# First context's projections between the halves of the last output product, and its keys' softmax ahead of the last gate

## The reference

```
x = layernorm(x + rwkv(x))              # 4 layers: time mix (wkv recurrence), then channel mix
x = layernorm(x + attention(x, ctx))    # 16 heads of 16 channels, no T x S matrix
x = layernorm(x + experts(x))           # 8 experts, dense, weighted by two softmaxes

# channel mix of a layer
kf = square(relu(xk @ Wck.T));  x = x + sigmoid(xr @ Wcr.T) * (kf @ Wcv.T)

# attention
q = softmax(heads(x @ Wq.T + bq));  k = softmax(heads(ctx @ Wk.T + bk));  v = heads(ctx @ Wv.T + bv)
kv = k.T @ v;  D_inv = 1 / sum(q * sum(k))
out = (q + (q @ kv) * D_inv) @ Wp.T + bp
```

## Time and profile before

| | us |
|---|---|
| median of 3 runs | 1799.88 |
| lowest and highest | 1799.08, 1801.06 |
| the profiled execution | 1800.33 |
| its span in the profile | 1798.3 |
| busy in the span: PE, DVE, ACT | 1711.9, 1222.4, 981.0 |

### The profile page before, as it was taken

The page is one execution under the profiler, slowest core; times in us unless marked ns, Lnnn a source line. Parts: engine busy times, 40 slices in busy tenths (PEclk is TensorE's granted clock), DMA queues, the critical chain, the costliest instruction groups (busy, mean ns, idle before and its releaser), DMA issues.

```text
span 1798.3 us, 25765 instructions
## 1 busy us (share of the span) xinstructions
PE 1711.9 (95%) x9740; PEld 1467.2 (82%) x9740; DVE 1222.4 (68%) x1900; ACT 981.0 (55%) x1514; POOL 17.5 (1%) x41
## 2 busy tenths in 40 slices
PE   3699999999999998999999999999999999999997
PEld 1377777778777787988899988999899989998897
DVE  7999999999999857998544444545444444444455
ACT  5788998898999873444533333333333333333333
POOL 0000000000000000000000000000000000000000
PEclk9799999999999999999999999999999999999999
DMA  5501110020001002211111101110010101120001
GB/s 150 87 1 30 24 59 18 18 68 27 18 18 41 1 29 91 68 47 42 47 36 36 36 1 35 35 35 2 33 35 35 35 0 35 35 76 0 1 1 42
DMA packets 37497, 64.23 MB, mean 36 GB/s; under 512 B 3271, under 2 KB 21549, under 8 KB 36397
## 3 DMA queue, kind: packets, MB, share of 16 engines
q1 hardware_dynamic: 34620, 55.47, 9.5%
q0 software_dynamic: 2800, 7.73, 2.8%
HBM read 59.53 MB, written 3.67 MB: 35 GB/s over the span
## 4 chain that ended last, share of the span: by engine, by line
PE 76%; DVE 12%; ACT 8%; issue 2%; DMA 0%; SPq 0%; ACTq 0%; DVEq 0%
PE fbank L2035 34%; PE fbank L2057 17%; PE pair L870 5%; PE pair L845 5%; PE pair L894 5%; PE pair L855 2%; PE pair L880 2%; PE proj L1503 2%; ACT xn L636 1%; ACT kf L660 1%; ACT kfh L662 1%; ACT kf L658 1%; PE pair L835 1%; DVE pp L390 1%; PE qbanks L1542 1%
## 5 line engine op out<-in xcount | busy, mean ns | idle before, releaser
L1846 DVE TENSOR_TENSOR hf<-sil,fbank 128x512 f32<-128x512 f32 (+1 forms) x256 | 159.0, 621 | 475.5 <-PE fbank L2035 421.7
L1961 ACT ACTIVATE sil<-fbank 128x512 f32<-128x512 f32 (+1 forms) x256 | 139.4, 544 | 614.9 <-PE fbank L2035 614.9
L2035 PE MATMUL fbank<-xh,wh 128*128 128x512 f32 (+1 forms) x1024 | 289.8, 364 | 1.2 <-ACT sil L1961 1.2
L2035 PE MATMUL fbank<-xl,wh 128*128 128x512 f32 (+1 forms) x1024 | 288.9, 363 | 0.0
L2035 PE MATMUL fbank<-xh,wl 128*128 128x512 f32 (+1 forms) x1024 | 288.9, 364 | 0.0
L2057 PE MATMUL fbank<-wl,hh 128*128 128x256 f32 x896 | 250.5, 280 | 0.0
L2057 PE MATMUL fbank<-wh,hh 128*128 128x256 f32 x896 | 250.4, 279 | 0.0
L2057 PE MATMUL fbank<-wh,hl 128*128 128x256 f32 x896 | 250.3, 279 | 0.0
L2035 PEld LDWEIGHTS fbank<-xl,wh 128*128 128x128 f32 x1024 | 184.5, 189 | 30.7
L2035 PEld LDWEIGHTS fbank<-xh,wl 128*128 128x128 f32 x1024 | 184.5, 189 | 30.3
L2035 PEld LDWEIGHTS fbank<-xh,wh 128*128 128x128 f32 x1024 | 180.6, 189 | 27.7 <-ACT sil L1961 1.6
(11 more groups left out here) (243 smaller groups left out, 2985.7 us busy)
## 6 DMA issues: line engine op xcount, KB each, us to landing
raw<-in_w_gate SPq DMA_DIRECT2D x16, 512.0 KB, 3.8
raw<-in_w_up SPq DMA_DIRECT2D x16, 512.0 KB, 4.7
raw<-in_w_down SPq DMA_DIRECT2D x16, 512.0 KB, 5.6
raw<-in_w_ck SPq DMA_DIRECT2D x4, 1024.0 KB, 7.3
raw<-in_w_cv SPq DMA_DIRECT2D x4, 1024.0 KB, 7.6
wcvl<-in_w_cv POOLq DMA_DIRECT2D x6, 512.0 KB, 5.5
raw<-in_ctx_t SPq DMA_DIRECT2D x4, 750.0 KB, 5.7
ct<-in_ctx_t SPq DMA_DIRECT2D x4, 750.0 KB, 5.0
```

The costliest lines, as they stand in the source:

```text
L1846: dve.tensor_tensor(hf[i][:, 0:w], sil[i][:, 0:w], banks(e, t, f)[1][:, 0:w], ALU.mult).then_inc(hf_ready, 1)
L1961: act.activation(sil[f % 2][:, 0:w], banks(e, t, f)[0][:, 0:w], ACT.Silu).then_inc(sil_ready, 1)
L2035: ins = pe.matmul(banks(e, t, f)[k][:, 0:w], m[h][:, o:o + P], a[:, b, columns(c)], start=i == 0, stop=i == 3 * CB - 1)
```

## The change

On PE, the projections of context 0 and the small product for the output bias become a function `first_context`, called between the two halves of the last output product, behind a wait for ACT's last relu. On DVE, `k_arguments(0)`, `output_bias` and `k_normalise(0)` become `first_keys`, called ahead of `gate_channel(15)`. The loop over contexts leaves these out for context 0. The lists of ACT, SP and POOL are the same instruction by instruction.

```diff
--- before.py
+++ after.py
@@ -281,7 +281,7 @@
             load_context(sp, io, g["ct"], g["ct_in"], 0)
 
         def vector(dve):
-            attention_begins, attention = g["attention"]["vector"](dve)
+            attention_begins, context_keys, attention = g["attention"]["vector"](dve)
             steps = [0]
 
             def did(ins):
@@ -543,6 +543,8 @@
                     wkv_denominator(s + 1)
                 if valid(s - 1):
                     low_kf(s - 1, 3)
+                if s == STEPS:
+                    context_keys()
                 if valid(s):
                     rsqrt(2, s)
                     set_shift(2)
@@ -825,6 +827,7 @@
             attention()
 
         def tensor(pe):
+            first_context, attention = g["attention"]["tensor"](pe)
             pe.wait_ge(const_set, 12)
 
             def turn(k, m, banks):
@@ -923,6 +926,10 @@
                     pe.wait_ge(wlo_ready["cv"], 32 * (m // GROUPS) + 16)
                     pe.wait_ge(cth_ready, m + 1)
                     channel_out(m, (0, 1))
+                if s == STEPS:
+
+                    pe.wait_ge(relu_done, 4 * STEPS)
+                    first_context()
                 m = s + 2
                 if valid(m):
                     if m and s < 1:
@@ -982,6 +989,7 @@
                     hidden(m, 2)
                     pe.wait_ge(relu_done, 4 * m + 1)
                     hidden(m, 3)
+            attention()
 
         return {"gpsimd": gpsimd, "sync": sync, "vector": vector, "scalar": scalar, "tensor": tensor}
 
@@ -1292,16 +1300,20 @@
                 split_rows(0, 2)
                 low_context(1)
 
+            def first_keys():
+
+                k_arguments(0)
+                output_bias()
+                k_normalise(0)
+
             def groups():
 
                 times_up, low_h, combine_arguments, combine_weights, experts = g["expert"]["vector"](dve)
                 dve.wait_ge(mask_set, 3)
                 for n in range(B):
                     i, c1, c2 = stage(n)
-                    k_arguments(n)
-                    if n == 0:
-                        output_bias()
                     if n:
+                        k_arguments(n)
                         block_diagonals(n - 1)
                     if i == 0 and c1 is not None:
                         add_input(c1)
@@ -1309,7 +1321,8 @@
                         q_normalise(c1)
                     if i == 3 and c2 is not None:
                         add_attention(c2)
-                    k_normalise(n)
+                    if n:
+                        k_normalise(n)
                     if n + 2 < B:
                         low_context(n + 2)
                     if i == 0 and c1 is not None:
@@ -1352,7 +1365,7 @@
                 combine_weights()
                 experts()
 
-            return begin, groups
+            return begin, first_keys, groups
 
         def scalar(act):
             def v_out(s):
@@ -1601,68 +1614,74 @@
 
             gate_up, experts = g["expert"]["tensor"](pe)
             last = GROUPS - 1
-            pe.wait_ge(const_set, 6)
-            project_values(0)
-            project_rest(0)
-            pe.wait_ge(w_in, 48)
-            for b in range(CB):
-                ins = pe.matmul(kvp[0:2, 0:C], bv[:, b, :], wp[:, b, :], start=b == 0, stop=b == CB - 1)
-            ins.then_inc(pbias_done, 1)
...
+
+            def first_context():
+                pe.wait_ge(const_set, 6)
+                project_values(0)
+                project_rest(0)
+                pe.wait_ge(w_in, 48)
+                for b in range(CB):
+                    ins = pe.matmul(kvp[0:2, 0:C], bv[:, b, :], wp[:, b, :], start=b == 0, stop=b == CB - 1)
+                ins.then_inc(pbias_done, 1)
+
+            def groups():
+                for n in range(B):
...
+            return first_context, groups
 
         return {"gpsimd": gpsimd, "sync": sync, "vector": vector, "scalar": scalar, "tensor": tensor}
 
@@ -2140,7 +2159,6 @@
             @block.tensor
             def _(pe):
                 rwkv["tensor"](pe)
-                attention["tensor"](pe)
 
 def lay_out(inputs):
```

More of the change, by code:

```diff
@@ L1603, in tensor @@
             last = GROUPS - 1
-            pe.wait_ge(const_set, 6)
-            project_values(0)
-            project_rest(0)
-            pe.wait_ge(w_in, 48)
-            for b in range(CB):
-                ins = pe.matmul(kvp[0:2, 0:C], bv[:, b, :], wp[:, b, :], start=b == 0, stop=b == CB - 1)
-            ins.then_inc(pbias_done, 1)
[L1611 to L1628, removed]
-                        project_values(n + 1)
[L1630 to L1662, removed]
@@ L1663, in tensor @@
-            pe.wait_ge(g["logit_ready"], 1)
-            route(pe, kvp, g, LATE)
-            experts()
+            def first_context():
[8 more added lines that the diff above has]
+                for n in range(B):
+                    i, c1, c2 = stage(n)
+                    if n + 1 < B and i in (1, 2):
+                        project_values(n + 1)
+                    if i == 1 and c1 is not None:
+                        pe.wait_ge(xt_ready, c1 + 1)
+                        tokens_out(qbanks, xt, wq, 1, q_done)
+                    if i == 2 and c2 is not None:
+                        project_out(c2)
+                    if n in TURNS:
+                        turn_x2(TURNS.index(n))
+                    if i == 3 and c1 is not None:
+                        if n - 1 in TURNS:
+                            pe.wait_ge(g["x2t_ready"], TURNS.index(n - 1) + 1)
+                        pe.wait_ge(q_ready, c1 + 1)
+                        turn(qbanks, q[c1 % 2], q_turned)
+                    if n + 1 < B:
+                        if i in (0, 3):
+                            project_values(n + 1)
+                        project_rest(n + 1)
+                    if i == 0 and c2 is not None:
+                        attend(c2)
+                    if n == B - 1:
+                        gate_up(0, 0, 0)
+                        gate_up(0, 0, 1)
+                    if i == 0 and c2 is not None:
+                        pe.wait_ge(den_read, c2 + 1)
+                    keys_values(n)
+                    if i == 1 and c2 is not None:
+                        turn_out(c2)
+                    if i == 0 and c1 is not None:
+                        pe.wait_ge(x1_ready, c1 + 1)
+                        if c1:
+                            pe.wait_ge(qt_ready, c1)
+                        turn(qbanks, x[:, c1 * G:(c1 + 1) * G, :], x1_turned)
+                turn_x2(last - 1)
+                attend(last)
+                gate_up(0, 0, 2)
+                turn_out(last)
+                gate_up(0, 0, 3)
+                project_out(last)
+                gate_up(0, 1, 0)
+                gate_up(0, 1, 1)
+                pe.wait_ge(g["wrt_in"], 16)
+                pe.wait_ge(g["x2t_ready"], last)
+                pe.wait_ge(den_read, GROUPS)
+                route(pe, kvp, g, EARLY)
+                turn_x2(last)
+                gate_up(0, 1, 2)
+                gate_up(0, 1, 3)
+                pe.wait_ge(g["x2t_ready"], GROUPS)
+                pe.wait_ge(g["logit_ready"], 1)
+                route(pe, kvp, g, LATE)
+                experts()
```

## The result

| | before | changed |
|---|---|---|
| median, us | 1800.31 (13 runs) | 1804.16 (13 runs) |
| lowest and highest | 1799.08, 1801.87 | 1802.11, 1805.49 |
| ratio, 95% interval | | 1.0018, 1.0011 to 1.0026 |
| profiled execution, its span | 1800.33, 1798.3 | 1805.09, 1803.0 |

The account below looks back on a forecast made before the run. PE bounds nearly everywhere; behind the seam all hangs on the token transposition. add_input at 688.40 plus 6.43 us put it +0.99 later, clock 0; against the median 1799.88 that gave 1800.9 us, range 1798.6 to 1803.9.

Parts of the forecast that it names:

- The signs that were named for right: At the seam: block at 669.8, L1598 without wait, DVE idle some 4 us for xin, issue 684.10, transposition 694.8, one PE hole.
- the clock at 0.50 beyond 699: PE's granted clock still at half after 699 us, behind the seam; named as the sign of the second rival.
- The block on PE: Between the halves of the last output product: context 0's projections take 5.75 us, and the wait for the relu costs nothing.
- DVE's side: Ahead of the channel mix's gate: the division adds 0.83 us, so the turn back (PE's transposition of the gated product) moves 6.58.
- SP's side: Load of xin behind the residual addition: issued 6.58 us later, lands after 4.3, so add_input starts 3.3 us later, at 688.40.
- The path to the transposition: From add_input to the first token transposition on PE: 6.43 us, the division's 2.33 being out of it; transposition +0.99 us.
- A: Measured piece from the last output product's first matmul to the token transposition; the forecast moved that transposition by +0.99 us.
- The clock at the seam: PE's low clock behind the hole: same 1.64 us loss as before, so 0; bounds -1.64 and +3.9.
- the long hole holds the clock down: Rival, query projections behind the transposition: clock stays low, up to 3.9 us more, total 1804.8; chance 0.16.
- The clock further on: From the transposition to the kernel's end: no term; the end was to move by as much as the transposition.
- C: Measured piece from the keys' product of context 2 to the end of the span; the forecast had no term for it.
- the load is no bound: Rival at the seam: add_input does not wait for xin, transposition 3.3 us earlier, clock another -1.64, total 1794.9; chance 0.06.

Follow-up runs that it names:

- divide_late: Changed kernel with the division of context 0's keys' softmax moved behind the residual addition on DVE; ratio 1.0013 to the kernel before.
- early_x: Changed kernel with the loads of xin issued behind the last output product, not behind the residual addition; ratio 0.9976 to the kernel before, 0.9978 repeated.
- x_apart: Changed kernel with chunk 0 of xin loaded long ahead into a free staging tile; ratio 0.9978 to the kernel before.
- before_early_x: Kernel before with the loads of xin issued behind the last output product; ratio 1.0007 to the unaltered kernel before.
- before_warm: Kernel before with 13 and 8 extra matmuls, results unused, in PE's two holes at the seam; ratio 0.9998 to the unaltered kernel before.
- again_before_warm: before_warm once more, unaltered, for a second profile; ratio 1.0001 to the kernel before.

## Why the prediction was right, and where its size failed

The signs that were named for right all came, counted from the last output product. So did one that was named for wrong, the clock at 0.50 beyond 699. The measured median, 1804.16, lies 0.3 us above the range of 1798.6 to 1803.9; by the ratio, 1.0018 on the 1799.88 from which the prediction starts, it is 1803.1 and within. So the chain of waits was right, and two terms of the clock that stood at nothing make most of the loss.

- **The block on PE.** Right. It takes 5.67 us (5.75 forecast), its wait for the last relu costs nothing, and the keys' product waits no more.
- **DVE's side.** Right in kind. The division holds the gate, by 0.62 us by divide_late, not 0.83. The turn back moved by 6.41 us, not 6.58.
- **SP's side.** Right, and the step that decides. The load was issued 6.41 us later relative to the output product, took 4.19 us to `add_input` where 4.3 was forecast, and DVE waited 4.22. early_x and x_apart show it by taking the wait away, before_early_x by finding nothing to take. The estimate of 3.05 us, worked out from the fit for GpSimd's path in the Trainium skill (DMA: Bandwidth & Descriptors, "Anatomy of one DMA"), does not hold for this load from SP: 4.19 and 4.56 here, near the 4.3 in the row of before.
- **The path to the transposition.** 6.44 us from `add_input` (689.54 to 695.98), 6.43 forecast. A moved by 0.72 and 1.04; the forecast was 0.99.
- **The clock at the seam.** This is the term that was mis-sized. I wrote "The coming hole is longer, and I take the same loss again: 0". It cost 1.15 to 1.29 us more, since it stayed low 6.3 and 6.0 us into the work and not 3.6. The rival "the long hole holds the clock down" met its own sign, 0.50 more than 4 us after PE resumed, at a third of the 3.9 it was given. Its mechanism is not what the windows show: the low stretch was as long as before, 6.8 us, and only began later against the transposition. The clock term should have stood at a value between the bounds that I had named.
- **The clock further on.** The sum had no term for it. The prediction said that whatever moves the transposition moves the end by as much, and that holds only while the later falls of the clock stay as they are. C grew by 1.3 us in both profiles, and before_warm shows that 1.6 us gained at the seam can come back as 1.4 lost there.
- **The rival that the load is no bound** is refuted for this kernel, but its conditions were made by early_x: 1794.9 was worked out for it, and it came to 0.22 to 0.24% under the kernel before, about 1796 on the prediction's base.

The version to keep is early_x: it is the change as given, with two loads behind the product that frees their tile instead of behind the addition three steps on, 0.24% (0.14 to 0.34) faster than before, 0.22% (0.13 to 0.31) in the repetition. By the order and sizes of the allocations in the code, which is an estimate, the tile of `xin` lies over `kfh`, which the last output product is the last to read.

## What to carry to other kernels

When work is moved ahead of the end of a stage, look at what waits for that end on a queue that the diff does not touch: here a transfer had 3.3 us of cover, the move took it away and more, and the change was a loss until the transfer waited for what frees its tile and nothing else. Compare where the load is issued with the last reader of the memory it writes; a semaphore that stands for "the stage is over" is often several steps later than that. And when a hole on PE moves or grows, look where PE's low clock will lie against the work behind it, and not only how long the hole is: here one hole of 5.9 us cost 1.5 more, another 2.8, and one of 3.6 cost 2.6. Keep its price as a range.

## What was not expected of the hardware

In this kernel a gain on PE's path was taken back by the clock far away from it. before_warm and again_before_warm were 1.6 us ahead at the seam and had a fall of PE's clock at about 850 us, 1.4 to 1.5 us, that the unaltered kernel does not have; the total stayed at 0.9998 and 1.0001. The start of the last output product, ahead of which these kernels run the same instructions but for a load or two, lay between 663.8 and 667.3 us over the 14 profiles. Five of them have a fall of the clock at about 620 us, which by what a fall costs in C is about 1.5 us of the start in each, an estimate; the rest of the spread was not traced. So a single profile of two kernels can't be compared by its span to better than about 3 us, while A repeats to 0.01 us in the kernel before.
